# Second FFN of a routed macaron block: rows scattered to token order block by block, weight copies split over three engines

## What is computed

```python
x = x + 0.5 * ffn(layernorm(x)); x = x + attn(layernorm(x)); x = x + 0.5 * ffn(layernorm(x))
# ffn:
logits = xt @ gate_w.T + gate_b
top_v, top_i = jax.lax.top_k(logits, 2)
h0, h1 = xt @ w0[e].T + b0[e], xt @ w1[e].T + b1[e]
y[e] = (h0 * silu(h1)) @ w2[e].T + b2[e]
out = (softmax(top_v)[:, :, None] * y[top_i]).sum(axis=1)
```

## Time and profile before

| what | value |
|---|---|
| median of 3 runs | 855.84 us (855.53 to 857.2) |
| the profiled execution's own time | 854.1 us |
| its span | 852.4 us |
| busy: TensorE, VectorE, ACT, GpSimd | 519.1, 548.1, 380.2, 495.0 us |
| first FFN's blocks | about 122 to 238 us |
| attention with the second router | about 240 to 634 us |
| second FFN's blocks | about 650 to 764 us |
| gathers, sums and stores at the end | about 764 to 852 us |

### The profile page before, as it was taken

The page is one execution under the profiler, slowest core; times in us unless marked ns, Lnnn a source line. Parts: engine busy times, 40 slices in busy tenths (PEclk is TensorE's granted clock), DMA queues, the critical chain, the costliest instruction groups (busy, mean ns, idle before and its releaser), DMA issues. The chain is left out here.

```text
span 852.4 us, 14942 instructions
## 1 busy us (share of the span) xinstructions
PE 519.1 (61%) x4422; PEld 397.1 (47%) x4422; DVE 548.1 (64%) x1745; ACT 380.2 (45%) x824; POOL 495.0 (58%) x568
## 2 busy tenths in 40 slices
PE   2222219999911578888888888888405999960000
PEld 2121218999900234554555555554205999960000
DVE  5546617888731787899999999883423888851222
ACT  1101107887700036666666666667104778750000
POOL 2767773655558865655766755224451566537775
PEclk9999999999965559999999999999656999995555
DMA  7201132333211111111211211100012233312222
GB/s 264 102 38 41 42 109 73 95 100 94 76 50 53 50 45 58 58 59 50 62 58 57 71 46 60 54 17 25 28 43 81 88 100 95 95 62 65 77 83 71
DMA packets 51564, 59.54 MB, mean 70 GB/s; under 512 B 11052, under 2 KB 45804, under 8 KB 50668
## 3 DMA queue, kind: packets, MB, share of 16 engines
q1 hardware_dynamic: 42732, 41.52, 15.2%
q0 software_dynamic: 8192, 16.79, 6.3%
q10 hardware_dynamic: 560, 0.27, 0.1%
HBM read 30.80 MB, written 27.26 MB: 68 GB/s over the span
## 5 line engine op out<-in xcount | busy, mean ns | idle before, releaser
L957 DVE TENSOR_REDUCE attn_nm<-ps 128x2 f32<-128x512 f32 x256 | 169.4, 684 | 38.9 <-PE ps L659 36.7
L517 POOL CAST experts_w<-w_table 128x1536 fp32r x78 | 118.5, 1519 | 109.6 <-ACT experts_y L456 103.1
L766 ACT ACTIVATE attn_pt<-ps 128x512 f32<-128x512 f32 x256 | 147.5, 597 | 70.9 <-PE ps L643 68.6
L280 POOL DMA_INDIRECT x_rows<-route_xn,route_rows x128 | 129.9, 1015 | 57.2 <-issue 33.3
L659 PE MATMUL ps<-attn_ka,attn_qa 128*128 128x256 bf16 x512 | 106.5, 295 | 60.3 <-DMA attn_qa<-kq_pieces 30.5
L643 PE MATMUL ps<-attn_qa,attn_ka 128*128 128x256 bf16 x512 | 99.0, 277 | 4.4 <-ACT attn_pt L766 2.4
L399 PE MATMUL ps<-experts_x_hi,experts_w 128*128 128x256 f32 x312 | 95.3, 305 | 5.0 <-DVE experts_x_lo L482 1.2
L476 DVE SCALAR_TENSOR_TENSOR experts_act<-ps,experts_b,experts_silu 128x256 f32<-128x256 f32 x156 | 68.3, 479 | 39.6 <-PE ps L401 37.7
L401 PE MATMUL ps<-experts_x_hi,experts_w 128*128 128x256 f32 x312 | 89.1, 286 | 0.0
L400 PE MATMUL ps<-experts_x_lo,experts_w 128*128 128x256 f32 x312 | 88.9, 285 | 0.0
L659 PEld LDWEIGHTS ps<-attn_ka,attn_qa 128*128 128x128 bf16 x512 | 39.8, 101 | 96.0 <-DVE attn_nm L957 51.4
(11 more groups left out here) (165 smaller groups left out, 1169.3 us busy)
## 6 DMA issues: line engine op xcount, KB each, us to landing
experts_x<-x_rows SPq DMA_DIRECT2D x78, 128.0 KB, 2.0
y_rows<-experts_y_tokens SPq DMA_DIRECT2D x78, 128.0 KB, 1.7
kq_pieces<-attn_kqp SPq DMA_DIRECT2D x16, 192.0 KB
x_rows<-route_xn,route_rows POOLq DMA_INDIRECT x128, 2.2
x_rows<-zeros SPq DMA_DIRECT2D x16, 128.0 KB, 1.7
out<-x_tokens SPq DMA_DIRECT2D x16, 128.0 KB, 1.7
x_tokens<-x SPq DMA_DIRECT2D x7, 256.0 KB, 6.4
attn_ka<-kq_pieces SPq DMA_DIRECT2D x16, 96.0 KB
```

The lines of the kernel that those rows point to most:

```text
L280: nc.gpsimd.indirect_dma_start(out=x_rows[:, :], out_offset=to, in_=xn[:, g % RX, t, :], in_offset=None).then_inc(sent[g % RX], 16)
L517: nc.gpsimd.tensor_copy(m["w"][:, j % WR], w_table[:, bass.ds(e, 1), :].rearrange("p a w -> p (a w)")).then_inc(w_ready, 1)
L766: nc.scalar.activation(pt[:, g % 2, j, :], ps[:, SBK[h % 2], :], ACT.Exp, scale=SCALE).then_inc(exp_done, 1)
L957: nc.vector.tensor_reduce(nm[:, qc, 2 * pair:2 * pair + 2], ps[:, SA[k], :].rearrange("p (j t) -> p j t", t=S), AX.X, ALU.max, negate=True ...
```

## The change

In the second FFN a block's output rows no longer go to `y_rows` to be gathered at the end. Each row of `x_rows` gets two more columns: the token's first expert, and twice the token's number. VectorE makes from them, for each block, the row of a new DRAM tensor `y_tokens` (token order, two rows a token) where each output row belongs, and GpSimd sends the block's rows there with two indirect DMAs. At the end SP reads `y_tokens` back with 16 plain loads. GpSimd copies a third of a block's weights (w1) and the biases, ACT w2, VectorE w0. The first FFN keeps its stores, gathers and copies.

The core of the diff:

```diff
+FIRST, TWICE, XCOLS = P, P + 1, P + 2
-    x_rows = nc.dram_tensor("x_rows", [ROWS, P], F32)
+    x_rows = nc.dram_tensor("x_rows", [ROWS, XCOLS], F32)
+    y_tokens = nc.dram_tensor("y_tokens", [2 * TOKENS + DUMP, P], F32)
@@ router
     def dve_pick(dve, g):
         dve.wait_ge(topf_done, g + 1)
+        if g >= GROUPS:
+            marks = xn[:, g % RX, :, FIRST:XCOLS]
+            first = g % GROUPS * TG
+            nc.vector.tensor_copy(marks[:, :, 0:1], top_f[:, :, 0:1]).then_inc(marked, 1)
+            nc.vector.tensor_copy(marks[:, :, 1:2], const["twice"][:, first:first + TG].unsqueeze(2)).then_inc(marked, 1)
@@ experts
+    IR = 6
+    W_AHEAD, AT_ONCE = 2, 13
...
+        wait(pe, w0_ready, j - LISTED + 1)
+        wait(pe, w2_ready, j - LISTED + 1)
...
     def act(act, turn):
         js, own = steps(turn, AHEAD, Y_LAG)
+        if turn:
+            act.wait_ge(route["list_ready"], 6)
+        es = {}
         for j in js:
+            n = j + W_AHEAD
+            if turn and n in own:
+                if n not in es:
+                    es = {i: expert_of(act, i) for i in own[n - own.start:n - own.start + AT_ONCE]}
+                act_w2(act, n, es[n])
             if j in own:
                 for k in range(CH):
                     act_silu(act, j, k)
...
+    def dve_to(dve, j):
+        dve.wait_ge(x_in[j % XR], 16 * (j // XR + 1))
+        dve.wait_ge(w_ready, 2 * (j + 1))
+        wait_out(dve, j - IR)
+        marks = m["x"][:, j % XR, :, FIRST:XCOLS]
+        wait(dve, to_ready, j - LISTED - 1)
+        nc.vector.scalar_tensor_tensor(out=m["row"][:, j % 2].unsqueeze(2), in0=marks[:, :, 0:1],
+                                       scalar=m["b"][:, j % WR, BE:BE + 1], in1=marks[:, :, 1:2],
+                                       op0=ALU.not_equal, op1=ALU.add).then_inc(row_found, 1)
+        dve.wait_ge(row_found, j - LISTED + 1)
+        nc.vector.scalar_tensor_tensor(out=m["to"][:, j % IR, :], in0=const["dumped"], scalar=float((j - LISTED) * SLOTS),
+                                       in1=m["row"][:, j % 2], op0=ALU.add, op1=ALU.min).then_inc(to_ready, 1)
...
+    def pool_w1(pool, j):
+        e = expert_of(pool, j)
+        wait(pool, y_copied, j - WR + 1)
+        wait(pool, to_ready, j - WR - LISTED + 1)
+        nc.gpsimd.tensor_copy(*part(j, e, W1H)).then_inc(w_ready, 1)
+        nc.gpsimd.tensor_copy(m["b"][:, j % WR], b_table[...]).then_inc(w_ready, 1)
+
+    def act_w2(act, j, e):
+        wait(act, y_ready, j - WR + 1)
+        nc.scalar.activation(*part(j, e, W2H), ACT.Copy).then_inc(w2_ready, 1)
+
+    def dve_w0(dve, j, e):
+        wait(dve, h0_ready, j - WR + 1)
+        nc.vector.tensor_copy(*part(j, e, W0H)).then_inc(w0_ready, 1)
+
+    def pool_scatter(pool):
+        pool.wait_ge(route["list_ready"], 6)
+        for j in range(LISTED, LISTED + WR - 1):
+            pool_w1(pool, j)
+        for j in range(LISTED, 2 * LISTED):
+            if j + WR - 1 < 2 * LISTED:
+                pool_w1(pool, j + WR - 1)
+            pool.wait_ge(rows_done, j + 1)
+            pool.wait_ge(to_ready, j - LISTED + 1)
+            for i in range(2):
+                to = bass.IndirectOffsetOnAxis(ap=m["to"][:, j % IR, i:i + 1], axis=0)
+                nc.gpsimd.indirect_dma_start(out=y_tokens[:, :], out_offset=to, in_=m["y_tokens"][:, j % YR, i, :],
+                                             in_offset=None).then_inc(y_sent[j % YR], 16)
@@ first_ffn, VectorE
             nc.vector.tensor_scalar(const["upto"], const["upto"], 0.0, None, ALU.is_ge).then_inc(upto_done, 1)
+            dve.wait_ge(zeros_out, 16 * NB)
+            nc.vector.memset(no_rows[:, :, TWICE:XCOLS], NOBODY).then_inc(upto_done, 1)
+            nc.vector.tensor_copy(b_table[:, :, BE:BE + 1], const["iota"].unsqueeze(2)).then_inc(upto_done, 1)
             route["dve_norm"](dve, 1)
@@ first_ffn, SP
             sp.wait_ge(zeros_made, 1)
-            sp.dma_start(x_rows[E * REGION:ROWS, :].rearrange("(s p i) d -> p s (i d)", p=P, i=2),
-                         zeros[:].unsqueeze(1).broadcast_to([P, SPARE, 2 * P])).then_inc(zeros_out, 16)
             for b in range(NB):
                 sp.dma_start(kq_dram[...], ...).then_inc(zeros_out, 16)
+            sp.wait_ge(upto_done, 3)
+            sp.dma_start(x_rows[E * REGION:ROWS, :]..., no_rows...).then_inc(zeros_out, 16)
@@ second_ffn
-            blocks["pool"](pool, 1)
-            blocks["all_out"](pool, 1)
-            pool.wait_ge(route["found"], 2)
...
-                        nc.gpsimd.indirect_dma_start(out=y[:, tile, r, :], out_offset=None, in_=y_rows[:, :],
-                                                     in_offset=route["y_offset"](1, tile, r)).then_inc(gathered[b // 2], 16)
+            blocks["pool_scatter"](pool)
...
-            route["dve_find"](dve, 1)
             blocks["dve"](dve, 1)
             for b in range(NB):
-                dve.wait_ge(gathered[b // 2], 16 * 8)
+                dve.wait_ge(y_in[b // 4], 16 * 4)
...
-            blocks["sp"](sp, 1)
+            blocks["sp_second"](sp)
+            blocks["all_out"](sp, 1)
+            for b in range(NB):
+                rows = y_tokens[b * 2 * S:(b + 1) * 2 * S, :].rearrange("(p i) d -> p (i d)", i=4)
+                sp.dma_start(y[:, b].rearrange("p t r d -> p (t r d)"), rows).then_inc(y_in[b // 4], 16)
```

More of the change, by code:

```diff
@@ L276, in pool_send @@
         pool.wait_ge(rows_ready, g + 1)
+        if g < RX:
+            pool.wait_ge(marks_blank, 1)
+        wait(pool, marked, 2 * (g - GROUPS + 1))
         for t in ts:
@@ L355, in experts @@
     x_in, y_out = [sem(f"x_in{i}") for i in range(XR)], [sem(f"y_out{i}") for i in range(YR)]
+    y_sent = [sem(f"y_sent{i}") for i in range(YR)]
+    w0_ready, w2_ready, to_ready = sem("w0_ready"), sem("w2_ready"), sem("to_ready")
+    row_found = sem("row_found")
     w_ready, xT_ready, xhi_done, xlo_done = sem("w_ready"), sem("xT_ready"), sem("xhi_done"), sem("xlo_done")
@@ L376, in allocate @@
         sb("y_tokens", [P, YR, 2, P])
+        if turn:
+            sb("row", [P, 2, 2])
+            m["to"] = late.enter_context(nc.sbuf_tensor("experts1_to", [P, IR, 2], U32))
     def steps(turn, before, after):
@@ L381, in steps, with wait_out @@
         return range(own.start - before, own.stop + after), own
+    def wait_out(eng, j):
+        first = len(range(j % YR, LISTED, YR))
+        uses = j // YR + 1
+        wait(eng, y_out[j % YR], 16 * min(uses, first))
+        wait(eng, y_sent[j % YR], 32 * (uses - first))
     def pe_x(pe, j):
@@ L492, in dve_rows @@
         dve.wait_ge(yT_ready, j + 1)
-        wait(dve, y_out[j % YR], 16 * (j // YR))
+        wait_out(dve, j - YR)
         nc.vector.tensor_copy(m["y_tokens"][:, j % YR], ps[:, YT, 0:SLOTS].rearrange("p (i d) -> p i d", d=P)).then_inc(rows_done, 1)
+    def dve_to(dve, j):
[10 more added lines that the diff above has]
+                                       in1=m["row"][:, j % 2], op0=ALU.add, op1=ALU.min).then_inc(to_ready, 1)
     def dve(dve, turn):
         js, own = steps(turn, AHEAD, ROW_LAG)
+        es = {}
         for j in js:
+            n = j + W_AHEAD
+            if turn and n in own:
+                if n not in es:
+                    es = {i: expert_of(dve, i) for i in own[n - own.start:n - own.start + AT_ONCE]}
+                dve_w0(dve, n, es[n])
             if j in own:
@@ L505, in dve, with pool_weights @@
                 dve_rows(dve, j - ROW_LAG)
+            if turn and j in own:
+                dve_to(dve, j)
             if j in own:
                 dve_lo(dve, j)
-    def pool(pool, turn):
-        pool.wait_ge(route["list_ready"], 3 * (turn + 1))
-        js, own = steps(turn, 0, 0)
-        for j in js:
-            i = j - own.start
-            e = pool.value_load(route["listed"][i:i + 1, turn, 1:2], min_val=0, max_val=E - 1)
+    def pool_weights(pool):
+        pool.wait_ge(route["list_ready"], 3)
+        for j in range(LISTED):
+            e = pool.value_load(route["listed"][j:j + 1, 0, 1:2], min_val=0, max_val=E - 1)
             wait(pool, y_copied, j - WR + 1)
@@ L528, in sp, with sp_x, sp_first @@
         sp.wait_ge(tails, 16 * E * (turn + 1))
-        js, own = steps(turn, XR, ROW_LAG)
-        for j in js:
-            n = j + XR
-            if n in own:
-                at = sp.value_load(route["listed"][n - own.start:n - own.start + 1, turn, 0:1], min_val=0, max_val=ROWS - SLOTS)
-                wait(sp, xT_ready, n - XR + 1)
-                sp.dma_start(m["x"][:, n % XR], x_rows[bass.ds(at, SLOTS), :].rearrange("(p i) d -> p i d", i=2)).then_inc(x_in[n % XR], 16)
+    def sp_x(sp, j):
+        turn, i = divmod(j, LISTED)
+        at = sp.value_load(route["listed"][i:i + 1, turn, 0:1], min_val=0, max_val=ROWS - SLOTS)
+        wait(sp, xT_ready, j - XR + 1)
+        wait(sp, to_ready, j - XR - LISTED + 1)
+        sp.dma_start(m["x"][:, j % XR], x_rows[bass.ds(at, SLOTS), :].rearrange("(p i) d -> p i d", i=2)).then_inc(x_in[j % XR], 16)
```

(6 more changed lines are left out.)

101 lines of the change are left out of this document (61 added, 40 removed).

## The result

| what | before | after |
|---|---|---|
| median | 855.68 us (855.31 to 857.2, 4 runs) | 1083.59 us (1080.82 to 1087.01, 4 runs) |
| span of the profiled execution | 852.4 | 1083.1 |
| mean granted clock over the span | 0.874 | 0.809 |

What follows compares the result with a forecast made beforehand. TensorE was taken to set the pace of the second FFN's blocks, with GpSimd's gathers after them. 854.1 + 17.7 + 1 + 1.5 + 266.8 - 52.0 = 1089.1, plus 1.7 for the median: 1091 us, range 1050 to 1130.

Steps and rivals of the forecast that it cites:

- the steps: Second FFN, blocks 42 to 77: 35 steps grow from 2.78 to 10.4 us, each one full turn of waits; +266.8 us.
- the router: Second FFN's router: 16 more small VectorE instructions, 0 to 2.7 us, taken as +1 us.
- Rival 1: Second FFN's steps: TensorE's clock stays high or comes back early, total 1021, or 1056 for half of it; chance 0.15.
- The start: Before the first scatter: VectorE waits for SP's 16 zero stores, delaying router and scatters; +17.7 us, between 15 and 20.
- Steps 41 and 42: Second FFN: these two steps already have ACT's wait for its w2 copy; +1.5 us, 0 to 3.
- the end: From block 77's first matmul: gathers give way to scatters, plain loads and sums, 44.7 us against 96.7; -52.0 us.
- Rival 2: Second FFN: VectorE's copies hold up GpSimd's scatters, 0.69 us a step for one, total 1115, or 1139 for both; chance 0.12.
- the ring: Second FFN: waits from TensorE through ACT, VectorE and GpSimd back to TensorE, one block per turn, 10.4 us at the lower clock.
- Rival 3: Second FFN: GpSimd's copies run ahead of scatters, 3.2 us a step, total 839, faster; deciding step about 3.7; chance 0.03.
- The register loads: Second FFN, ACT and VectorE: 13 loads at a time, 7.5 us, hidden in a pause; uncovered up to 15 us in all.

Runs made afterwards that it cites:

- e1: Changed kernel with GpSimd's w1 and bias copies issued one block earlier, ahead of the scatters: 946.76 us against 890.99 for the kernel before (1.063).
- e2: Changed kernel with ACT's w2 copy moved to the end of ACT's step: 1057.62 us against 890.99 for the kernel before (1.188).
- e3: Changed kernel with both the edits of e1 and e2: 904.23 us against 890.99 for the kernel before (1.015).
- e4: Changed kernel with VectorE's wait for the zero stores moved behind the router: 1106.06 us against 890.99 for the kernel before (1.242).
- e8: Kernel before with rows of 130 columns and two small VectorE copies per group in the second router: 862.71 us against 855.11 (1.009).
- e9: Kernel before with rows of 130 columns alone, without the two small router copies: 894.79 us against 893.4 (1.002).
- e12: e7 with w0 copied by ACT together with w2, and the two small router copies later: 857.09 us against 893.4 for the kernel before (0.9595).
- e6: Changed kernel with the edits of e1, e2 and e4, and one register load a step instead of 13: 833.4 us against 855.11 before (0.974).
- e7: e6 with five weight slots in place of four: 819.49 us against 855.11 for the kernel before (0.959).

## Why the prediction was right, point by point

The spans differ by 230.7 us and the forecast terms add up to 235.0. That is nearer than the terms are: the steps were put 8.1 us too high and the router 6.2 too low, and that these cancel is luck.

**The steps (+266.8 forecast, +258.7 measured).** The mechanism is shown, not only fitted: e1 and e2 each loosen one link, by moving copies in one queue and nothing else, and e3 brings back 81% of what the steps lost. The links, one by one: TensorE to `y_ready` 4.1 where 4.6 was forecast, because the clock did come back, at the end of each burst, as the 0.71 of 859 to 862 shows; ACT and VectorE together 2.75 (861.48 to 864.23) against 2.45, because ACT starts 0.14 after `y_ready` and because the second product after silu, which the prediction laid beside ACT's work, stands in VectorE's queue ahead of x_lo (x_hi ends at 863.25, x_lo starts at 863.49); GpSimd 3.28 against 3.25 (864.23 to 867.51), and 0.11 to TensorE. So 10.27 in place of 10.4: two errors of 0.5 and 0.3 us, of opposite sign. Rival 1 (the clock) is true in this small part and in no more. The last step was 7.9 us, since no w2 copy stood in front of it; the prediction had counted a full one.

**The start (+17.7, measured +16.4).** Right in mechanism, shown by e4. The zeros landed by 28.2, not 29.5: the 16 stores were issued in 6.65 us in place of 7.62, and the last landed about 1.1 us after that, not 2.2. (The prediction's own terms, 20.04 + 7.62, end at 27.7 and not at the 27.3 that it goes on with.)

**The router (+1, measured +7.2).** This is the term that was mis-sized. The prediction gave the 16 copies at most their own 2.7 us and then less, "since part of the attention waits for other engines". e8 puts 7.6 us on them by the medians and 5.3 by its trace, and e9 takes the longer rows out as a cause. What turns 2.6 us of VectorE into twice that and more is open: e12 does not decide it, and the sums of waits before and after don't either, since several grew (ACT's for TensorE's scores from 68.6 to 74.5 us, TensorE's for `attn_qa` from 30.5 to 32.5). The 0.6 more in the first FFN has no experiment.

**Steps 41 and 42 (+1.5, measured +0.5), the end (-52.0, measured -53.0).** The sum of the end's parts held to 1 us, and each of the two instants that were checked to 0.2.

**Rival 2, the scatters behind VectorE's copies.** The Trainium skill ("SBUF — State Buffer", section "SBUF: two separate sides") says that a float32 copy from SBUF to SBUF on VectorE keeps GpSimd from writing the descriptors of its DMAs. The runs agree, but either side can pay. In the changed kernel w0's copy starts 0.64 us into the scatter: the scatter takes its 0.98, and the copy waits, 0.56 us in place of 0.43, which costs nothing since VectorE has time. In e6 the copy starts 0.62 to 0.68 us into the scatter and takes its 0.43, and in all blocks but one it is the scatter that grows, to 1.40 and more. So the order of the starts does not decide it; what does is not shown. In three blocks of e3 the copy starts 0.46 us in, and the scatter grows too (timeline):

```profile
759.16 1.40 POOL L622 DMA_INDIRECT y_tokens<-experts_y_tokens,experts_to  x1 [0.16 <-issue]
759.62 0.42 DVE L608 CAST experts_w<-w_table 128x512 fp32r x1
```

1.40 is 0.98 and the whole 0.42 of the copy. In e6 the mean of 23 scatters was 1.20 us for this, while e7's 24 took 0.97. So it cost 0.44 us a step in e6, where GpSimd has no slack, and nothing in the ring of the changed kernel. Rival 2 was rightly a side case here, and its price was too high: 0.69 an instruction where 0.44 was measured, and two instructions where only the copy counts. The low part of the product, VectorE's instruction with two inputs, left the scatter around it at 0.97 (e7, from 720.50, the low part from 720.70 to 721.39).

**Rival 3, the ring not closed (839).** Wrong for the change as it is. e6 is the kernel that it describes, at 3.6 us a step in place of 3.2, and with the start repaired besides: its 833.4 lies near 839 by luck. With the start's 16.2 us back in it would be some 850 (an estimate), a gain of under 1%. The point from which it decides was put at 3.7 us a step. With the measured terms it is 2.78 + (53.0 - 16.4 - 7.2 - 0.8) / 38 = 3.5 (0.8 being the two small terms of the first FFN and of the way to block 39), and e3, with 3.65 and two long steps, is indeed still slower than before (1.015).

**The register loads**, costed at nothing with the pause of 7 us as their cover and at 15 us without it: both held (0.2 and under 0.1 us in the two steps of the changed kernel, 13.5 us and some 3 behind them in e3). One at a time, e6, they hide behind queued work.

## What to carry to other kernels

Busy times bound a pipeline only if nothing in it waits for itself: before an edit that mixes a producer's instruction (a weight copy) with a consumer's (a scatter) in one in-order queue, write down which block each stands behind and follow the waits until they return. The length of that turn divided by the number of blocks it spans is the step, so a second block of lead about halved it here. Then look for the second ring: of the 259 us lost in the steps, GpSimd's lead alone gave back 175 and ACT's place alone 56, together 211. And when a stall goes, charge what it hid.
